# Row statistics for the second attention: where and in what portions they are taken

## The reference

```python
x = x + _L0_xattn_ref(_layernorm(x, axis=-1), ctx_2048, ...)
x = x + _L0_ffn_ref(_layernorm(x, axis=-1), L0_ffn_w_gating, L0_ffn_w_linear)
x = x + _L1_xattn_ref(_layernorm(x, axis=-1), ctx_2048, ctx_2048, L1_xattn_gamma)
x = x + _L1_ffn_ref(_layernorm(x, axis=-1), L1_ffn_gate_w, ...)
```

```python
def _layernorm(x, axis=-1, eps=1e-05):
    m = jnp.mean(x, axis=axis, keepdims=True)
    v = jnp.var(x, axis=axis, keepdims=True)
    return (x - m) / jnp.sqrt(v + eps)
...
    qk = jnp.einsum('bhdq,bhdl->bhql', qh, kh) * scale
    sm = jax.nn.softmax(qk, axis=-1)
    ret = jnp.einsum('bhql,bhdl->bhdq', sm, vh)
```

## Time and profile before

| | |
|---|---|
| three timed runs | 752.54, 754.99 (median), 756.26 us |
| the profiled execution | 751.65 us, span 749.9 us |
| busy: TensorE | 704.2 us, 94% |
| VectorE | 568.7 us, 76% |
| ScalarE | 409.5 us, 55% |
| GpSimd | 365.1 us, 49% |
| L1774, the 120 reductions of units 1 to 15 | 141.1 us on VectorE |
| L1050, L1052, L1054, all 16 of each | 10.9, 2.9, 2.5 us |
| L1064, all 16 | 9.2 us |

### The profile page before, as it was taken

How to read it: one execution, slowest core, us unless ns; L and a number is a source line. 1 busy time by engine, 2 the same in 40 slices (tenths; PEclk the granted TensorE clock), 3 DMA queues, 4 the chain that set the end, 5 groups by cost and what they waited for, 6 DMA issues and landing times.

```text
span 749.9 us, 15945 instructions
## 1 busy us (share of the span) xinstructions
PE 704.2 (94%) x5053; PEld 312.2 (42%) x5053; DVE 568.7 (76%) x1108; ACT 409.5 (55%) x764; POOL 365.1 (49%) x356
## 2 busy tenths in 40 slices
PE   4999999999999999898999999999998898999995
PEld 2444544444444444222233333333334554555552
DVE  5698999796876869687988899899967665555553
ACT  2555454763646547256877877777776433222221
POOL 5666555113011031265577657876574663343433
PEclk9999999999999999979999999999999999999999
DMA  8999980017365397234334433553566999999975
GB/s 309 388 139 217 304 333 0 1 40 263 114 213 203 113 341 280 61 101 114 99 92 116 113 108 114 146 155 84 175 207 129 166 195 138 123 137 131 129 112 71
DMA packets 114188, 117.61 MB, mean 157 GB/s; under 512 B 54840, under 2 KB 78264, under 8 KB 113856
## 3 DMA queue, kind: packets, MB, share of 16 engines
q1 hardware_dynamic: 103008, 94.48, 43.5%
q0 software_dynamic: 10384, 22.02, 18.1%
q10 hardware_dynamic: 720, 0.13, 0.1%
HBM read 43.61 MB, written 59.56 MB: 138 GB/s over the span
## 4 chain that ended last, share of the span: by engine, by line
PE 22%; DMA 14%; issue 10%; DVE 6%; ACT 2%; POOL 2%; POOLq 1%; SPq 1%; DVEq 0%; ACTq 0%
PE l_b L1540 7%; DMA out<-t_room,t_tag 6%; PE l_sm L1560 6%; PE l_pv L1552 4%; DMA out<-l_pvs,t_tag 4%; DVE l_negm L1774 2%; DMA out<-l_sums,t_tag 2%; PE l_a L1479 2%; PE l_b L1492 1%; ACT t_room L1682 1%; DVE h_negm L1774 1%; SPq L1042 1%; PE l_b L1529 1%; DMA out<-l_r,t_tag 1%; POOLq L1230 1%
## 5 line engine op out<-in xcount | busy, mean ns | idle before, releaser
L1682 ACT ACTIVATE t_room<-l_b 128x512 f32<-128x512 f32 x256 | 140.1, 600 | 37.7 <-PE l_b L1540 35.5
L1774 DVE TENSOR_REDUCE l_negm<-l_a 128x2 f32<-128x1024 f32 x64 | 75.2, 1219 | 9.9 <-PE l_a L1479 9.9
L1157 PE MATMUL l_a<-w1h,h_stack 128*128 x312 | 76.2, 313 | 3.5 <-issue 2.3
L1186 ACT ACTIVATE l_stack<-l_stack 128x352 f32<-128x352 f32 x39 | 19.4, 497 | 104.3 <-DVE l_stack L1210 100.6
L1774 DVE TENSOR_REDUCE h_negm<-l_a 128x2 f32<-128x1024 f32 x56 | 65.9, 1219 | 5.5 <-PE l_a L1479 5.1
L1560 PE MATMUL l_sm<-t_room,ones_f 128*32 128x512 f32 x512 | 68.0, 606 | 1.1
L1552 PE MATMUL l_pv<-t_room,l_vt 128*32 128x512 f32 x512 | 67.7, 603 | 0.5 <-issue 0.2
L852 PE MATMUL ps_st<-f_xt,wg 128*128 128x512 fp8e4 x256 | 65.7, 379 | 0.0
L852 PE MATMUL ps_r<-f_xt,wg 128*128 128x512 fp8e4 x256 | 65.7, 379 | 0.0
L1001 POOL TENSOR_TENSOR X<-X,f_y 128x512 f32<-128x512 f32 x16 | 20.7, 1295 | 79.2 <-ACT f_y L902 79.2
L1240 POOL DMA_INDIRECT out<-t_room,t_tag x20 | 31.7, 1585 | 48.0 <-DVE t_room L1225 32.4
(11 more groups left out here) (302 smaller groups left out, 1575.4 us busy)
## 6 DMA issues: line engine op xcount, KB each, us to landing
slots_x<-empty SPq DMA_DIRECT2D x8, 2376.0 KB, 11.1
slots_x<-empty SPq DMA_DIRECT2D x7, 2112.0 KB, 17.0
h_stack<-h_wide SPq DMA_DIRECT2D x96, 64.0 KB
l_stack<-h_wide SPq DMA_DIRECT2D x96, 64.0 KB
f_stage<-in_w SPq DMA_DIRECT2D x8, 704.0 KB, 7.1
f_stage<-in_w SPq DMA_DIRECT2D x8, 512.0 KB
h_wide<-in_ctx SPq DMA_DIRECT2D x16, 256.0 KB
l_vt<-in_ctx_t SPq DMA_DIRECT2D x16, 256.0 KB, 3.2
```

The lines of the kernel that those rows point to most:

```text
L1157: mm = pe.matmul(self.HP[i % 2][:, 0:self.H], T.xt[i % T.AHEAD][:, xp * self.FC + f, :], self.w1[wp][:, bass.ds(e, 1), f * self.H:(f + 1) ...
L1682: act.activation(weights_at(u, c, h)[:, :], B[t % 2][:, :], ACT.Exp, scale=SCALE).then_inc(b_ok, 1)
L1774: dve.tensor_reduce(negm[u % 2][:, 2 * half:2 * half + 2, j], A[half][:, :, :], AX.X, ALU.max, negate=True)\
```

## The change

The statistics are kept in arrays with a place for each of the 16 tiles. `statistics` takes a range of tiles and makes only L1050 and L1052; `variances` adds eps for several tiles in one instruction, and `power` takes the roots of several in one. Tiles 0 to 3 are done at the end of the feed-forward's group 1, tiles 4 to 7 at the end of group 2 (on VectorE behind the split, on GpSimd behind the group's four additions), tiles 8, 9 and 10 at m = 0, 8 and 11 of the last group, with their roots together in front of the last group's additions. Tiles 11 to 15 stay in the attention, one by one and in the old places. So in the attention the statistics of tile 2 at its start and those of tiles 3 to 10 in units 0 to 7 are gone, and the roots with them. On GpSimd the wait for the root of tile 2 becomes one for its own earlier subtraction.

```diff
--- before.py
+++ after.py
@@ -925,6 +925,7 @@
                         dve.tensor_tensor(EW.w2[1][0:rows, e, cols], stage2[0:rows, cols], EW.w2[0][0:rows, e, cols], ALU.subtract)\
                             .then_inc(lo2_ok, 1)
 
+            SOON_AT = (0, 8, 11)
             LATE = (1, 2, 3, 4, 5, 6, 9, 10, 12, 13, 14, 15)
 
             def group(g, more):
@@ -955,18 +956,24 @@
                         split(2 * g, m - (HC - 6))
                     if not more and m in LATE:
                         split(2 * g + LATE.index(m) // 6, LATE.index(m) % 6)
-                    if not more and m == 0:
-                        F.statistics(dve, X, 0)
+                    if not more and m in SOON_AT:
+                        u = (g - 1) * G + SOON_AT.index(m)
+                        dve.wait_ge(res_ok, u + 1)
+                        F.statistics(dve, X, u, u + 1)
                     if not more and m == 7:
                         F.queries(dve, X, 0)
-                    if not more and m == 11:
-                        F.statistics(dve, X, 1)
+                    if not more and m == SOON_AT[-1]:
+                        F.variances(dve, (g - 1) * G, (g - 1) * G + len(SOON_AT))
                 dve.wait_ge(h8_ok, g * HC + HC)
                 if more:
                     for part in range(6):
                         split(2 * g + 1, part)
                     if g == 0:
                         last.vector(dve, HC)
+                    else:
+                        dve.wait_ge(res_ok, g * G)
+                        F.statistics(dve, X, (g - 1) * G, g * G)
+                        F.variances(dve, (g - 1) * G, g * G)
                 else:
                     for k in range(2 * F.TC):
                         dve.wait_ge(F.a_ps, k + 1)
@@ -989,17 +996,20 @@
                     last.gpsimd(pool, last.batches)
                 if not more:
                     pool.wait_ge(res_ok, g * G)
+                    pool.wait_ge(F.rstd_ok, (g - 1) * G)
                     pool.memset(F.stack[F.M0:F.M0 + 1, 0, :, :], 1.0).then_inc(F.set_ok, 1)
                     pool.wait_ge(F.set_ok, 1)
-                    F.power(pool, neg_half, 0)
                     F.low_keys(pool, F.parts, 0)
                     F.low_queries(pool, F.parts, 0)
-                    F.power(pool, neg_half, 1)
+                    F.power(pool, neg_half, (g - 1) * G, F.SOONER)
                 for r in range(G):
                     pool.wait_ge(y_ok, g * G + r + 1)
                     xr = X[:, bass.ds(g * G + r, 1), :]
                     pool.tensor_tensor(xr, xr, y[r % 2][:, :], ALU.add).then_inc(res_ok, 1)
-
+                if more and g:
+                    F.power(pool, neg_half, (g - 1) * G, g * G)
+
+            assert (NG - 2) * G + 3 == F.SOONER
             groups(pool, group)
 
     return range(ops.stat_ok.num, lo2_ok.num + 1)
@@ -1008,7 +1018,9 @@
 class FirstUnit:
 
 
-    def __init__(self, nc, st, D, DH):
+    SOONER = 11
+
+    def __init__(self, nc, st, D, DH, NT):
         HU, TC = P // DH, D // P
 
         def sb(name, shape, dt=F32):
@@ -1023,7 +1035,7 @@
         parts = [self.wide[:, 2 * k * D:2 * (k + 1) * D].bitcast(BF16).rearrange("p (n d) -> p n d", d=D) for k in range(2)]
         self.parts, self.parts1 = parts
         self.kf, self.qf = self.wide[:, 4 * D:5 * D], self.wide[:, 5 * D:6 * D]
-        self.st6, self.mv, self.veps, self.rstd = sb("st6", [P, 6]), sb("mv", [P, 2]), sb("veps", [P, 1]), sb("rstd", [P, 1])
+        self.st6, self.mv, self.veps, self.rstd = sb("st6", [P, 6]), sb("mv", [P, NT, 2]), sb("veps", [P, NT]), sb("rstd", [P, NT])
         self.negm = sb("negm", [P, HU, TC])
         self.mrow = sb("mrow", [HU * TC, P], BF16)
         self.kf_ok, self.stack_ok, self.row_in, self.set_ok = sem("kf"), sem("stack0"), sem("row0"), sem("set")
@@ -1045,23 +1057,26 @@
     def place_rows(self, sp, stack, mrow, row_in):
         sp.dma_start(stack[self.M0:self.M0 + 1, 1, :, :].rearrange("o h (j t) -> o (h j) t", t=P), mrow[:, :]).then_inc(row_in, 16)
 
-    def statistics(self, dve, X, u):
-        wait(dve, self.rstd_ok, u)
-        dve.bn_stats(self.st6[:, :], X[:, u, :]).then_inc(self.stat_ok, 1)
-        wait_apart(dve, (self.stat_ok, u + 1), (self.qf_ok, u))
-        dve.bn_aggr(self.mv[:, :], self.st6[:, :]).then_inc(self.aggr_ok, 1)
-        dve.wait_ge(self.aggr_ok, u + 1)
-        dve.tensor_scalar(self.veps[:, :], self.mv[:, 1:2], EPS, None, ALU.add).then_inc(self.veps_ok, 1)
+    def statistics(self, dve, X, first, last):
+        for u in range(first, last):
+            wait(dve, self.aggr_ok, u)
+            dve.bn_stats(self.st6[:, :], X[:, u, :]).then_inc(self.stat_ok, 1)
+            dve.wait_ge(self.stat_ok, u + 1)
+            dve.bn_aggr(self.mv[:, u, :], self.st6[:, :]).then_inc(self.aggr_ok, 1)
+
+    def variances(self, dve, first, last):
+        dve.wait_ge(self.aggr_ok, last)
+        dve.tensor_scalar(self.veps[:, first:last], self.mv[:, first:last, 1], EPS, None, ALU.add).then_inc(self.veps_ok, last - first)
 
     def queries(self, dve, X, u):
         dve.wait_ge(self.rstd_ok, u + 1)
         wait(dve, self.ql_ok, u)
-        dve.tensor_scalar(self.qf[:, :], X[:, u, :], self.mv[:, 0:1], self.rstd[:, :], ALU.subtract, ALU.mult).then_inc(self.qf_ok, 1)
-
-    def power(self, pool, neg_half, u):
-        pool.wait_ge(self.veps_ok, u + 1)
-        wait(pool, self.qf_ok, u)
-        pool.tensor_tensor(self.rstd[:, :], self.veps[:, :], neg_half[:, 0:1], ALU.pow).then_inc(self.rstd_ok, 1)
+        dve.tensor_scalar(self.qf[:, :], X[:, u, :], self.mv[:, u, 0:1], self.rstd[:, u:u + 1], ALU.subtract, ALU.mult).then_inc(self.qf_ok, 1)
+
+    def power(self, pool, neg_half, first, last):
+        pool.wait_ge(self.veps_ok, last)
+        pool.tensor_tensor(self.rstd[:, first:last], self.veps[:, first:last], neg_half[:, 0:last - first], ALU.pow)\
+            .then_inc(self.rstd_ok, last - first)
 
     def high_keys(self, act, parts, u):
         act.wait_ge(self.kf_ok, 16 * u + 16)
@@ -1975,7 +1990,6 @@
                 ht, from_ps = tiles.turned(dve, i)
                 dve.tensor_copy(ht, from_ps).then_inc(tiles.ht_ok, 1)
 
-            F.statistics(dve, X, 2)
             for j in range(EARLY):
                 maxima(1, j)
             dve.wait_ge(gam_ok, 16)
@@ -2006,8 +2020,9 @@
                 if u == NU - 1:
                     first_ends()
                     meeting_table(0, SOON, soon_passed, soon_skipped)
-                if u + 3 < NU:
-                    F.statistics(dve, X, u + 3)
+                if F.SOONER <= u + 3 < NU:
+                    F.statistics(dve, X, u + 3, u + 4)
+                    F.variances(dve, u + 3, u + 4)
                 if u + 2 < NU:
                     maxima(u + 2, 0)
                 if u:
@@ -2147,8 +2162,7 @@
 
             keys(1)
             queries(1)
-            F.power(pool, neg_half, 2)
-            pool.wait_ge(F.rstd_ok, 3)
+            pool.wait_ge(F.ql_ok, 2)
             pool.memset(stack[1][M0:M0 + 1, 0, :, :], 1.0).then_inc(set_ok, 1)
             pool.wait_ge(set_ok, 2)
             keys(2)
@@ -2183,8 +2197,8 @@
                     with_reciprocals(u - 1)
                 if u == 1:
                     keys(u + 3)
-                if u + 3 < NU:
-                    F.power(pool, neg_half, u + 3)
+                if F.SOONER <= u + 3 < NU:
+                    F.power(pool, neg_half, u + 3, u + 4)
                 if u >= 2:
                     low_rows(u - 2)
                 between(u, 2)
@@ -2295,7 +2309,7 @@
 
         EW = ExpertWeights(sb, D, H, E)
         first = ExitStack()
-        F = FirstUnit(nc, first, D, 32)
+        F = FirstUnit(nc, first, D, 32, NT)
         late = Room(EW.w1[0][:, 2:E, :].rearrange("p e k -> p (e k)").bitcast(F32))
         early = Room(*(part[:, :, :].rearrange("p e k -> p (e k)").bitcast(F32) for part in (EW.w1[1], EW.w2[0], EW.w2[1])))
         two = ExitStack()
```

## The result

The changed kernel took 757.94 us (median of 18 runs, 753.78 to 764.38), the kernel before 755.41 in the same comparison (18 runs, 751.18 to 759.66). The ratio is 1.0040, with a 95% interval of 1.0022 to 1.0057: 3.0 us slower, 1.7 to 4.3. Two further comparisons gave 1.0043 (1.0019 to 1.0067) and 1.0045 (1.0028 to 1.0062), so 3.2 and 3.4 us. The medians alone differ by less, by 2.5, 2.0 and 2.6 us. The forecast had 1.4 us of loss and 756.4 us.

A forecast was written before the change was run, and what follows sets the result against it. TensorE was taken to set the pace in the feed-forward and the attention's first units. Losses of 0.4, 0.1 and 0.88 us (units 3, 6, 7) sum to 1.4, giving 756.4 us; range 752.6 to 759.5.

The forecast's parts named there:

- The likeliest case: Whole kernel: a loss of 0.5 to 2.5 us, with 1.4 us as its value; chance 0.45.
- One of the prediction's own signs of being wrong: Feed-forward: the prediction is wrong if a product there starts to wait for VectorE; no size given.
- VectorE's freed time gains nothing.: Units 0 to 7: time freed by removed statistics becomes a longer wait for GpSimd's product; gain 0.
- The removed root lets `low_rows` in, 0.14 us ahead, and the normalisation takes some 1.57 us.: Units 3 to 7: GpSimd's subtraction starts first and blocks VectorE's normalisation, 0.88 us over its 0.69.
- Rival (b): Attention: the collision of `low_rows` and normalisation doesn't happen or is absorbed; 755.0 us, chance 0.25.
- In unit 3 it costs 0.4.: Attention unit 3: the second reduction ends late for the second half of TensorE's product; loss 0.4 us.
- Units 0 to 2 have no such pair.: Attention units 0 to 2: no collision of GpSimd's subtraction with VectorE's normalisation, so no loss charged.
- Units 4 and 5 absorb theirs, unit 6 loses 0.1, unit 7 loses 0.88.: Attention: slack takes the delay in units 4 and 5; 0.1 us lost in unit 6, 0.88 in unit 7.
- Rival (c): Attention units 3 to 7: all five carry the 0.88 us in full, 4.4 us; 759.4 us, chance 0.12.
- Start of the attention: 0.: Attention's start: removing tile 2's statistics and root gains 0; the 2.26 us stall stays.
- Added to the feed-forward: 0.: Feed-forward: added statistics and roots fit into idle gaps of VectorE and GpSimd; cost 0.
- rival (d): Feed-forward: the four-tile statistics blocks overrun their gaps by 2 to 3 us; 757.5 us, chance 0.06.

The follow-up runs named there:

- after: The changed kernel itself, against the kernel before; profiled three times, ratios 1.0040, 1.0043 and 1.0045.
- the kernel that has the attention as before: Changed kernel with idle GpSimd roots and idle VectorE statistics put back in units 0 to 7 and at the attention's start: 750.99 us, ratio 0.9996 to the kernel before.
- the kernel that keeps the attention's collisions: Changed kernel with only GpSimd's memset of ones moved, between the third and fourth addition of feed-forward group 2: 751.36 us, ratio 1.0011 to the kernel before.
- the full repair: Changed kernel with the memset moved and GpSimd waiting for VectorE's normalisation before `low_rows` in units 2 to 7: ratios 1.0032 and 1.0015 to the kernel before.

## Why the prediction was right or wrong

The time, 757.94, lies in the range, but that says little: the range took in no change at all as well. The likeliest case, a loss of 0.5 to 2.5 us with 1.4 as its value, had the mechanism and not the whole size, and none of the three terms of its sum came out as it stands. One of the prediction's own signs of being wrong came true: in the feed-forward a product of TensorE (L835, at 302.62) waits 0.69 us for VectorE, 0.61 and 0.68 in the other two executions. By its steps:

- *VectorE's freed time gains nothing.* Right: in no interval of any of these kernels was 14.75 us undercut up to unit 6, with the statistics gone or idle.
- *The removed root lets `low_rows` in, 0.14 us ahead, and the normalisation takes some 1.57 us.* Right to 0.01 us: 0.15 ahead and 1.56 in four of the five units. Rival (b), the collision absent, is out by the trace, and the kernel before without its roots shows that their absence is the cause in units 3 to 6.
- *In unit 3 it costs 0.4.* Wrong there: 14.75. `low_rows` started at 379.02, 0.31 ahead rather than 0.14, and so the normalisation took 1.40 and began earlier. Unit 2 had lost up to 1.17 us just before, which moved TensorE against GpSimd. In the kernel before without its roots, where unit 2 loses nothing, unit 3 has the case that was worked out, and it cost 0.56. The sum had put the slack too high by 0.15: by it the normalisation may end 0.96 us behind the copy (380.79 against 379.83), measured is 0.81.
- *"Units 0 to 2 have no such pair."* This is the first step that failed. The pair stood in the rows of unit 2 all along, 0.45 us apart and with 1.26 us for the normalisation, to which VectorE came late. After the change it is there 1.36 us early, begins on the release of GpSimd's product, `low_rows` 0.15 ahead of it, takes 1.57, and TensorE waits 0.74 in the middle of a product. Unit 2 lost 1.16, 0.59 and 1.15 us, in two of three executions more than any other unit. I had used these two rows as the price of a collision and not asked what the change does in the very unit that they come from. Here the root isn't all. The removed statistics let VectorE be early, so that the collision takes its full 1.56 us (0.94 with the roots alone left out). Whether that costs anything goes with the clock: with 1.71 us at 0.91 nothing was lost, and with 0.69 us at 1.00 and the statistics in place 0.30 was.
- *Units 4 and 5 absorb theirs, unit 6 loses 0.1, unit 7 loses 0.88.* Mis-sized. From unit 4 to 5 0.34 to 0.49 is lost, from 5 to 6 at most 0.05, from 6 to 7 0.46 to 0.76, from 7 to 8 0.44 to 0.51. With the roots alone left out units 4 and 5 do absorb theirs (0.01 and 0.05). In after the normalisation of unit 4 starts 0.25 to 0.41 us ahead of the copy rather than 0.69, and so ends 1.15 to 1.30 behind it. Unit 7 loses half of the 0.88, since its normalisation starts 0.48 to 0.56 us ahead of the copy there rather than 0.12. The prediction had kept each unit's start where it was. In the third execution of after TensorE's weight load for the second half waits too (PEld, unit 4):

```profile
398.41 0.09 PEld L1494 LDWEIGHTS l_a<-h_wide 32*128 32x128 bf16 x2 [0.40 <-DVE h_negm L1789]
```

- *The attention's sum, 1.4 us.* Measured 1.7 to 2.3 in the traces: the three executions of after take 92.36 us in the mean from unit 2 to 8. The three executions with 0.69 us in units 3 to 7 and the same clock take 90.40 in the mean, or 90.62 with the kernel that has the attention as before (91.28, with its other collision); all eight with 0.69 us there, whatever the clock, take 90.11. Rival (c), 4.4 us with 0.88 in every unit, is too much, though its mechanism (a late second reduction that TensorE can't make up) is what happened in the intervals that lost.
- *Start of the attention: 0.* Right at equal clock: 44.6 to 45.1 us in after, 44.6 to 44.8 in five other kernels with the full clock. The stall was 1.97 (2.47 and 2.13 in the other two), 2.26 before.
- *Added to the feed-forward: 0.* Half right. The four-tile blocks fit as worked out (2.79 and 2.39 us of cover left, 2.2 foreseen), L1063 took 0.69 even beside an addition, so rival (d) is out. The roots took 1.02 us rather than 1.2. What failed is the sentence that GpSimd's roots lie "where it waits for the next group": behind them in the queue stood a memset of 1.8 us, which met VectorE's cast in the kernel before already and meets more of it when it comes late. None of the rows of the prediction shows that memset. Its delay costs 0.75 us.
- *The chances.* The forecast's case was right in kind; 3.0 us lies between it and (c). The two terms from the traces are 1.7 to 2.3 and 0.75, in sum 2.5 to 3.0, against 3.0, 3.2 and 3.4 by the ratios and 2.5, 2.0 and 2.6 by the medians. That the forecast came within 1.6 us of the time is in part luck: it charged unit 3, which lost nothing, and charged nothing for units 2 and 4 and the feed-forward, which lost.

What stays open: the six measurements of changed kernels that have the attention mended lie at a mean of 1.0012, 0.9 us over the kernel before and not at it. In three of them the feed-forward's 0.75 us is still in, but the other three, without it, are the higher ones; and the kernel that keeps the attention's collisions has 1.0011 as well. So it is the traces that show both causes; that the repairs give back about 2.3 of 3.2 us is read from ratios of different comparisons, and most of those measurements have one repair only. Within one comparison the full repair gave back 0.22 and 1.66 us. Whether the rest is scatter or a cost of the changed program that the stretches don't show is not settled, nor which clock the executions without a profile had from 346 to 366 us.

## What to carry to other kernels

An instruction that you take out also spaced the two around it: ask of every removed one, off the critical path too, which instruction of its engine now starts earlier and what runs beside it on the engine that it shares something with. Ask the same of an instruction that you lengthen: all that is queued behind it moves, down to a memset that nobody waits for. Read the pair that gives you a price also as a place where the change acts. And when one unit of a loop loses time, the ones behind it no longer start where they did: work out their sums from the moved start.
